# A decoder layer in one kernel: a bias moved into a weight load, two loads swapped, and all instruction orders written anew

## The chip, the cores and the metric

The kernel runs on one core of a Trainium2 chip. A core has a matmul engine (TensorE, PE in the profile), a vector engine (VectorE, DVE), a scalar engine (ScalarE, ACT), a general engine (GpSimd, POOL) and a queue that issues transfers (SyncE, SP). Each runs its own list of instructions in order, and they meet only at semaphores. The metric is the device time of one launch in microseconds (us).

## What is computed

One post-norm decoder layer over 16 batches of 256 rows, 128 wide, in float32:

```python
# 1: linear attention, 16 heads of 8
q = elu(x @ Wq + bq) + 1;  k = elu(x @ Wk + bk) + 1;  v = x @ Wv + bv
k = k / sqrt(sum(k * k) + EPS)
attn = (q @ k.T) @ v                      # per head, no softmax
y = x + attn @ Wo + bo
x = layernorm(x + (layernorm(y) * gamma + beta))
# 2: cross-attention to 64 context rows, 16 heads of 64
p = softmax((x @ Wq_x)(ctx @ Wk_x).T * 64 ** -0.5)
x = layernorm(x + p @ (ctx @ Wv_x) @ Wo_x)
# 3: gated FFN, 352 wide, activations and weights rounded to FP4 by blocks of 16
h = silu(fp4(x) @ fp4(w_gate).T) * (fp4(x) @ fp4(w_up).T)
x = layernorm(x + fp4(h) @ fp4(w_down).T)
```

## The kernel before

The work of a batch b is cut into small calls, each one to sixteen instructions, defined once for their engine and then called in a list that is written out by hand, one list for each engine. Between the calls stand waits on semaphores. Since an engine does its list in order, the list decides which batches overlap.

**Set-up.** The query and key matrices of the cross-attention are folded with the context into one matrix M. `g_product` multiplies the weights per head (TensorE); `g_cut_high`, `g_keep_low` (VectorE) and `g_keep_high` (ScalarE) split the result GT into a high and a low part; `context_cut`, `context_low` (GpSimd) and `context_high` do it with the context, in two halves of 512 columns. `m_product(half, hd)` makes 3 matmuls for head hd and one half of the batches, 32 calls in all, over six PSUM banks; `m_keep` copies the banks away, in turn on ScalarE and VectorE. `hw_product` folds the value and output weights; `weights_...` round the FFN weights, `weights_transpose` and `keep_weights` bring them in place. VectorE's first call `biases` waits for the semaphore `aw_loaded`, which counts the loads of the key and value bias rows (`kv_bias`), the query bias (`bq_col`) and the attention weights (`w_attn`). `keep_warm(bank, n)` makes n matmuls whose result nobody reads; the first such call has n = WARM.

**Attention of batch b.** `project_kv` and `project_q` into bank A2; k's features by `k_exp` and `k_features`, then the inverse root in small steps (`k_sums` to `k_better`), `k_norm` on GpSimd; `kv_outer`, `keep_kvT`, `kv_project`, `keep_kvo`, `attn_out` in bank A1; `attn_residual` and two layer norms. Each layer norm goes `statistics`, `aggregate` (VectorE), `variance_eps`, `minus_mean`, `rstd_of`, `shift_of` (GpSimd), then a norm on ScalarE.

**Cross-attention.** `x1_transpose`, then for each half t of the rows `scores` into the two banks S, `score_max` (VectorE), `scores_shift` (TensorE adds the maximum into S), `softmax_exp` (ScalarE), `fold_halves` (GpSimd), `score_sums` and `score_reciprocals` (VectorE), `probabilities` (GpSimd), `p_transpose` into the banks TP, `keep_pT` (ScalarE) and `cross_out` into A2, with `values` and `keep_vo` once for a batch; then `cross_residual` and a layer norm, whose `cross_norm` writes into one of three x2 buffers and waits for the `ffn_residual` three batches back.

**FFN.** `x_max` to `x_rounded` and `x_dequantise` round the input, `xf_transpose`, `keep_xfT`; `gate_up(b, t)`, `gate_tanh`, `gate_times`, `gated` for each t; `h_max`, `h_reciprocal`, `h_scaled`, `h_magnitudes` (ScalarE), `h_rounded_up`, `h_rounded`, `h_dequantise` (GpSimd), `h_transpose`, `keep_hT`, `down` into A2, `ffn_residual`, layer norm, `store_out`. `gate_up(b, 1)` waits until `gated(b, 0)` has read its banks.

From scores(15, 1) on, TensorE's list reads: scores(15, 1), p_transpose(14, 1), gate_up(11, 0), cross_out(14, 0), h_transpose(10), gate_up(11, 1), p_transpose(15, 0), cross_out(14, 1), scores_shift(15, 1), values(15), xf_transpose(12), keep_warm(A2, 3), down(10), gate_up(12, 0), cross_out(15, 0), h_transpose(11), gate_up(12, 1), p_transpose(15, 1), cross_out(15, 1), xf_transpose(13), down(11), gate_up(13, 0), h_transpose(12), gate_up(13, 1), down(12), xf_transpose(14), gate_up(14, 0), keep_warm(F0, 8), gate_up(14, 1), xf_transpose(15), gate_up(15, 0), h_transpose(13), down(13), gate_up(15, 1), keep_warm(TP0, 4), h_transpose(14), down(14), keep_warm(TP0, 17), h_transpose(15), down(15).

## Time and profile before

| | |
|---|---|
| median of 3 runs | 390.3 us (390.25 to 391.2) |
| the profiled execution | 389.87 us |
| its span, first to last instruction | 387.9 us |
| TensorE busy | 357.9 us (92%), 2113 matmul records |
| VectorE busy | 295.1 us (76%) |
| GpSimd busy | 264.5 us (68%) |
| ScalarE busy | 248.7 us (64%) |

The time of the profiled execution and its span differ by what the launch adds before the first and after the last instruction. A float32 matmul is more than one record in the trace, and ends of matmuls are modelled, so the time that a call takes is read from its start to the start of the next. Transfers carry 26 GB/s over the span, most of it in the first 17 us.

### The profile page before, as it was taken

Reading aid. Unit: us, or ns where it says so; the run is one execution under the profiler, and the core shown is the slowest. Engines: PE = TensorE matmul, PEld = TensorE weight load, DVE = VectorE, ACT = ScalarE, POOL = GpSimd, SP = SyncE. Lnnn points to the kernel's source line nnn. Section 1 sums busy time; section 2 is a strip of 40 time slices with the busy share of each in tenths; the row PEclk is TensorE's granted clock in tenths of the full one; section 3 lists DMA queues with packets and bytes.
Section 4 is the critical chain, followed back from the end, with each engine's and each line's share of the span. In section 5 each row is a group of like instructions: output and inputs, shape, how many; then the busy total and the mean of one; then the engine's idle time right before and its main releaser. Section 6 shows DMA issues by size and latency. Waiting matters only on the chain.

```text
span 387.9 us, 7167 instructions
## 1 busy us (share of the span) xinstructions
PE 357.9 (92%) x2113; PEld 265.9 (69%) x2113; DVE 295.1 (76%) x814; ACT 248.7 (64%) x526; POOL 264.5 (68%) x441
## 2 busy tenths in 40 slices
PE   6499999899999999999999999999999999876782
PEld 6388766567767787577686778685776778664572
DVE  0879566757779897896766969797989788888881
ACT  0657667678668676766876696757666666545422
POOL 3501157998986979799877899788849676624232
PEclk9689999999999999999999999999999999999999
DMA  7810001101000011000000000000000000000000
GB/s 244 258 29 14 3 11 31 29 3 41 14 30 0 15 28 30 13 17 27 27 2 16 1 16 14 3 0 14 15 1 15 1 15 14 3 14 15 14 14 27
DMA packets 13280, 10.42 MB, mean 27 GB/s; under 512 B 1051, under 2 KB 12476, under 8 KB 13244
## 3 DMA queue, kind: packets, MB, share of 16 engines
q1 hardware_dynamic: 12668, 7.89, 7.0%
q10 hardware_dynamic: 576, 2.10, 1.5%
q8 instruction: 17, 0.28, 0.3%
q14 instruction: 19, 0.16, 0.1%
HBM read 7.88 MB, written 2.10 MB: 26 GB/s over the span
## 4 chain that ended last, share of the span: by engine, by line
PE 80%; issue 6%; DVE 5%; ACT 4%; DMA 2%; POOL 1%; SPq 0%; ACTq 0%; POOLq 0%; DVEq 0%
PE A L2589 15%; PE S L2562 14%; PE F L2604 8%; PE TP L2552 7%; PE TP L2580 7%; PE A L2619 4%; PE S L2571 4%; PE A L2513 3%; DMA w_attn<-in_attn_w 2%; PE TP L2491 2%; PE F L2491 2%; PE A L2537 2%; PE TP L2612 2%; PE A L2526 2%; PE S L2491 2%
## 5 line engine op out<-in xcount | busy, mean ns | idle before, releaser
L403 POOL TENSOR_TENSOR pe<-pe,srec 128x1024 f32<-128x1024 f32 x32 | 60.9, 1903 | 9.2 <-DVE srec L1704 9.2
L2589 PEld LDWEIGHTS A<-wvoT,wqkT 128*128 128x128 f32 x512 | 60.4, 192 | 4.4 <-ACT wqkT L987 1.7
L2589 PE MATMUL A<-wvoT,wqkT 128*128 128x128 f32 x512 | 62.2, 276 | 1.1 <-ACT wqkT L987 1.1
L2562 PE MATMUL S<-M,x1T 128*128 128x512 f32 x128 | 61.0, 599 | 0.8 <-ACT x1T L972 0.7
L397 POOL TENSOR_TENSOR fold<-pe 128x512 f32<-128x512 f32 x32 | 40.7, 1273 | 10.4 <-ACT pe L982 10.3
L1693 DVE TENSOR_REDUCE smax<-S 128x16 fp32r<-128x1024 f32 x32 | 39.0, 1218 | 3.6 <-PE S L2562 3.1
L2604 PE MATMUL F<-w_gu,xfT 128*128 128x352 f32 x112 | 38.0, 462 | 0.7 <-ACT xfT L995 0.6
L987 ACT ACTIVATE wqkT<-TP 128x1024 f32<-128x1024 f32 x32 | 32.7, 1023 | 8.7 <-PE TP L2580 8.5
L2562 PEld LDWEIGHTS S<-M,x1T 128*128 128x128 f32 x128 | 22.2, 190 | 21.0 <-issue 18.6
L982 ACT ACTIVATE pe<-S 128x1024 f32<-128x1024 f32 x32 | 32.7, 1021 | 6.0 <-PE S L2571 5.9
L413 POOL TENSOR_TENSOR hv<-hv,ham 128x704 f32<-128x704 f32 x16 | 22.2, 1387 | 17.5 <-DVE hv L1769 17.5
L2580 PE MATMUL TP<-ident,pe 128*128 128x128 f32 x256 | 33.3, 273 | 0.3 <-ACT wvoT L976 0.3
L2580 PEld LDWEIGHTS TP<-ident,pe 128*128 128x128 f32 x256 | 29.2, 141 | 4.7 <-issue 1.3
L2552 PE MATMUL TP<-HW,ctx_f 128*64 128x512 f32 x128 | 31.0, 605 | 0.0
L388 POOL TENSOR_TENSOR kn<-fk,ky 128x256 f32<-128x256 f32 x16 | 11.1, 694 | 27.5 <-DVE ky L1665 27.5
L2619 PEld LDWEIGHTS A<-w_dn,hT 128*128 128x128 f32 x192 | 23.1, 192 | 8.2 <-issue 5.6
L1698 DVE TENSOR_REDUCE ssum<-fold 128x16 f32<-128x512 f32 x32 | 21.8, 680 | 8.2 <-POOL fold L397 8.2
L2619 PE MATMUL A<-w_dn,hT 128*128 128x128 f32 x192 | 24.6, 278 | 3.4 <-ACT hT L1007 3.0
L381 POOL TENSOR_TENSOR xb<-x_sb,rows 128x512 f32<-128x512 f32 x16 | 20.4, 1273 | 10.5 <-DMA rows<-in_attn_rows 8.6
L2604 PEld LDWEIGHTS F<-w_gu,xfT 128*128 128x128 f32 x112 | 19.5, 190 | 9.0 <-issue 1.8
L2571 PE MATMUL S<-smax,ident_r 128*128 128x512 f32 x64 | 23.5, 448 | 1.8 <-DVE smax L1693 1.8
L954 ACT ACTIVATE x<-yx,shift_cross,rstd_cross 128x128 f32<-128x128 f32 x32 | 14.9, 489 | 11.7 <-DVE yf L1774 10.6
(188 smaller groups left out, 870.6 us busy)
## 6 DMA issues: line engine op xcount, KB each, us to landing
xT<-in_x_t SPq DMA_DIRECT2D x16, 128.0 KB, 2.1
x_sb<-in_x SPq DMA_DIRECT2D x16, 128.0 KB, 2.2
out<-yf SPq DMA_DIRECT2D x16, 128.0 KB, 1.8
M<-in_fw SPq DMA_DIRECT2D x1, 560.0 KB, 10.3
wqkT<-in_wq_t ACTq DMA_DIRECT2D x1, 512.0 KB, 4.3
wqkT<-in_wk_t ACTq DMA_DIRECT2D x1, 512.0 KB, 6.3
ctx_f<-in_ctx_t ACTq DMA_DIRECT2D x1, 512.0 KB, 7.9
wvoT<-in_wv_t ACTq DMA_DIRECT2D x1, 512.0 KB, 9.2
```

What stands on the lines that cost most here:

```text
L397: ge.tensor_tensor(by_head(fold[n % 2][:, :]), p4[:, :, 0, :], p4[:, :, 1, :], ALU.add).then_inc(fold_made, 1)
L403: ge.tensor_tensor(w, w, spread(srec[n % 2][:, :], HX, R), ALU.mult).then_inc(pn_made, 1)
L982: sc.activation(pe_[n % NPE][:, :], S[:, :], ACT.Exp, scale=SCALE).then_inc(pe_made, 1)
L987: sc.activation(pT[n % 2], TP[:, :].rearrange("p (a n) -> p a n", a=NJ), ACT.Copy).then_inc(pT_kept, 1)
L1693: ve.tensor_reduce(smax[n % 2][:, :], by_head(S[:, :]), AX.X, ALU.max, negate=True).then_inc(smax_made, 1)
L2552: last = te.matmul(TP[par * R:par * R + R, half * BANK:half * BANK + BANK], ctx_f[:, b * R:b * R + R], HW[:, par, 4 * half:4 * half + 4, : ...
L2562: last = te.matmul(S[:, half * BANK:half * BANK + BANK], x1T[b % 2][:, t * P:t * P + P], M[:, b // BH, HC * half:HC * half + HC, b % BH * ...
L2571: last = te.matmul(S[:, half * BANK:half * BANK + BANK], ident_r[:, :], spread(smax[n % 2][:, HC * half:HC * half + HC], HC, R), start=Fal ...
L2580: last = te.transpose(TP[:, j * P:j * P + P], pe_[n % NPE][:, j * P:j * P + P], ident[:, :])
L2589: last = te.matmul(A2[:, t * P:t * P + P], pT[n % 2][:, j, :], vo[b % 2][:, j, :], start=(j == 0), stop=(j == NJ - 1))
L2604: last = te.matmul(bk[:, 0:I], xfT[b % 2][:, t * P:t * P + P], w_gu[:, m, :], start=True, stop=True)
L2619: last = te.matmul(A2[:, t * P:t * P + P], hT[b % 2][:, t, k * P:k * P + P], w_dn[:, k, :], start=(k == 0), stop=(k == NK - 1))
```

## The change

The query bias is appended to the attention weights as a 513th column and `bq_col` becomes a view of it; its own load is gone. The load of the bias rows stands behind that of w_attn. `m_product` waits for the half of the context that it reads instead of for both. WARM is 18 instead of 12, and `keep_warm(F0, 6)` stands ahead of the first m_product. VectorE also gets a function `scores_shift` that nothing calls.

```diff
-def decoder_layer(nc, x, x_t, attn_w, attn_rows, bq_in, ctx_t, ...):
+def decoder_layer(nc, x, x_t, attn_w, attn_rows, ctx_t, ...):
-        w_attn = sb("w_attn", [P, 4 * P])
+        w_attn = sb("w_attn", [P, 4 * P + 1])
+        bq_col = w_attn[:, 4 * P:4 * P + 1]
-        bq_col = sb("bq_col", [P, 1])
-        WARM = 12
+        WARM = 18
-            sp.dma_start(kv_bias, attn_rows[0:2 * P].partition_broadcast(NBR)).then_inc(aw_loaded, 16)
-            sp.dma_start(bq_col[:, :], bq_in.rearrange("(p a) -> p a", a=1)).then_inc(aw_loaded, 16)
             load_xT(0)
             sp.dma_start(w_attn[:, :], attn_w).then_inc(aw_loaded, 16)
+            sp.dma_start(kv_bias, attn_rows[0:2 * P].partition_broadcast(NBR)).then_inc(aw_loaded, 16)
-            AW = 16 * 3
+            AW = 16 * 2
                 k = 2 * (hd // 2 // 4) + hd % 2
                 pe.wait_ge(g_high, k + 1)
                 pe.wait_ge(g_low, k + 1)
-                pe.wait_ge(c_high, 2)
-                pe.wait_ge(c_low, 2)
+                pe.wait_ge(c_high, half + 1)
+                pe.wait_ge(c_low, half + 1)
             project_kv(0)
-            pe.wait_ge(fk_made, 1)
-            project_q(0)
             pe.wait_ge(g_low, 2)
+            keep_warm(F0, 6)
             m_product(0, 0)
             pe.wait_ge(g_low, 2)
             m_product(0, 1)
+            pe.wait_ge(fk_made, 1)
+            project_q(0)
-        "attn_w": np.concatenate([i[f"L0_attn_W{n}"] for n in "kvqo"], axis=1),
+        "attn_w": np.concatenate([i[f"L0_attn_W{n}"] for n in "kvqo"] + [i["L0_attn_bq"][:, None]], axis=1),
-        "bq": i["L0_attn_bq"],
```

All five lists are written out in another order. They hold the same calls as before, apart from keep_warm: 44 such matmuls before, with WARM, and 57 after. The order of the loads of x and x_t changes from batch 5 on. Some of what moves: the second half of a batch's probabilities and its p_transpose, the attention calls of the first batches, which stood between the first m_products and now stand behind them, and the FFN calls of the first batches, which come later. The last steps of VectorE:

```diff
@@ VectorE, the last steps
             h_rounded_up(14)
+            ffn_residual(13)
             h_rounded(14)
-            ffn_residual(13)
-            statistics("ffn", 13)
             gate_times(15, 1)
-            aggregate("ffn", 13)
             gated(15, 1)
             h_max(15)
             h_reciprocal(15)
             h_scaled(15)
+            statistics("ffn", 13)
+            aggregate("ffn", 13)
+            h_rounded_up(15)
+            h_rounded(15)
             ffn_residual(14)
-            h_rounded_up(15)
             statistics("ffn", 14)
-            h_rounded(15)
             aggregate("ffn", 14)
```

From scores(15, 1) on, TensorE's list reads after the change: scores(15, 1), down(9), p_transpose(14, 1), gate_up(11, 0), scores_shift(15, 1), cross_out(14, 0), gate_up(11, 1), h_transpose(10), cross_out(14, 1), p_transpose(15, 0), down(10), p_transpose(15, 1), xf_transpose(12), cross_out(15, 0), gate_up(12, 0), cross_out(15, 1), gate_up(12, 1), xf_transpose(13), h_transpose(11), gate_up(13, 0), down(11), keep_warm(S0, 5), gate_up(13, 1), keep_warm(TP0, 7), h_transpose(12), down(12), xf_transpose(14), gate_up(14, 0), h_transpose(13), gate_up(14, 1), xf_transpose(15), gate_up(15, 0), down(13), keep_warm(S0, 3), gate_up(15, 1), keep_warm(TP0, 8), h_transpose(14), down(14), keep_warm(TP0, 10), h_transpose(15), down(15).

## Rows read from the trace of the kernel before

**Rows 1.** Busy time of each engine by stretch, with granted clock.

```profile
core 0: us, PE busy (x) PEld busy (x) DVE busy (x) ACT busy (x) POOL busy (x), PEclk, DMA share, GB/s
0.00:18.45 18.45, 9.54 (x64) 8.20 (x65) 7.47 (x21) 5.09 (x10) 8.18 (x27) 0.82 0.81 264
18.45:60.00 41.55, 41.34 (x215) 31.01 (x213) 29.57 (x76) 28.35 (x73) 10.04 (x20) 0.96 0.06 17
60.00:92.00 32.00, 29.09 (x150) 19.63 (x150) 22.07 (x75) 23.24 (x60) 29.44 (x45) 1.00 0.09 26
92.00:300.00 208.00, 207.99 (x1242) 152.62 (x1242) 169.84 (x487) 147.64 (x306) 174.83 (x278) 1.00 0.05 14
300.00:322.90 22.90, 22.32 (x134) 16.50 (x131) 19.86 (x49) 15.53 (x26) 16.28 (x28) 1.00 0.02 7
322.90:387.90 65.00, 47.67 (x319) 37.88 (x317) 46.33 (x111) 28.90 (x54) 25.76 (x47) 1.00 0.05 15
```

**Rows 2.** The chain that ended last, first 24 us: start, length, what.

```profile
2.17 8.73 DMA w_attn<-in_attn_w
```

**Rows 3.** Timeline of the first 22 us, all engines.

```profile
1.29 0.37 SPq L284 DMA_DIRECT2D bq_col<-in_bq  x1
...
2.12 4.36 PE L2626 MATMUL A<-ident 128*128 128x128 f32 x24 [2.12 <-POOL ident L350]
...
7.54 1.16 PE L2471 MATMUL F<-wqkT 64*128 64x128 f32 x16 [1.06 <-DMA wqkT<-in_wk_t]
...
10.92 0.15 DVE L1566 TENSOR_SCALAR bq_col<-bq_col 128x1 f32<-128x1 f32 x1 [9.79 <-DMA w_attn<-in_attn_w]
...
12.38 1.29 DVE L1586 TENSOR_SCALAR pe<-F 128x512 int32<-128x512 int32 x2
...
17.79 1.22 PE L2521 MATMUL A<-xT,w_attn 128*128 128x256 f32 x2 [2.87 <-DVE fk L1641]
...
18.45 3.12 PE L2491 MATMUL F<-ctx_r,GT 128*128 128x512 f32 x6
```

**Rows 4.** Stretches of 1 and 2 us; columns as in rows 1.

```profile
11.00:12.00 1.00, 0.00 (x0) 0.00 (x0) 0.90 (x6) 0.00 (x0) 0.00 (x0) 0.97 1.13 325
22.00:23.00 1.00, 1.00 (x5) 0.79 (x5) 0.79 (x3) 0.36 (x1) 0.00 (x0) 0.91 0.00 0
384.00:386.00 2.00, 0.00 (x0) 0.00 (x0) 0.00 (x0) 0.88 (x2) 0.57 (x2) 1.00 0.00 0
```

**Rows 5.** TensorE's waits, 56 to 92 us: total, times, longest.

```profile
PE S L2571 <- DVE smax L1693: 1.3, 2, 0.9
```

**Rows 6.** Waits of all engines, whole span.

```profile
ACT x L954 <- DVE yf L1774: 10.6, 5, 2.8
```

**Rows 7.** Timeline of TensorE near the end.

```profile
334.98 0.94 PE L2626 MATMUL A<-ident 128*128 128x128 f32 x6 [1.03 <-ACT xfT L995]
335.75 1.50 PE L2619 MATMUL A<-w_dn,hT 128*128 128x128 f32 x12
337.09 1.35 PE L2604 MATMUL F<-w_gu,xfT 128*128 128x352 f32 x4
338.27 1.95 PE L2589 MATMUL A<-wvoT,wqkT 128*128 128x128 f32 x16
340.06 0.82 PE L2612 MATMUL TP<-ident,hv 128*128 128x128 f32 x6
...
344.05 2.05 PE L2589 MATMUL A<-wvoT,wqkT 128*128 128x128 f32 x16 [1.11 <-ACT wqkT L987]
```

**Rows 8.** Timeline of the last 15 us, all engines.

```profile
374.46 3.96 PE L2626 MATMUL TP<-ident 128*128 128x128 f32 x34
374.67 0.42 DVE L1774 TENSOR_TENSOR yf<-A,x 128x256 f32<-128x256 f32 x1 [0.81 <-PE A L2619]
375.01 0.88 DVE L1764 SCALAR_TENSOR_TENSOR hv<-S,hv 128x704 f32<-128x704 f32 x1
...
376.20 0.87 DVE L1769 SCALAR_TENSOR_TENSOR hv<-S,hv 128x704 f32<-128x704 f32 x1
...
377.15 1.39 POOL L413 TENSOR_TENSOR hv<-hv,ham 128x704 f32<-128x704 f32 x1 [4.58 <-DVE hv L1769]
```

More of the change, by code:

```diff
@@ L2033, in _ @@
+            score_reciprocals(5, 1)
             cross_residual(4)
@@ new lines, in _ @@
+            gate_times(6, 0)
+            gated(6, 0)
+            q_features(15)
+            k_guess(15)
+            score_max(12, 0)
+            statistics("post", 13)
+            k_miss(15, 0)
+            gate_times(6, 1)
+            gated(6, 1)
+            h_max(6)
+            h_reciprocal(6)
+            h_scaled(6)
+            k_better(15, 0)
+            ffn_residual(5)
+            aggregate("post", 13)
+            statistics("ffn", 5)
+            h_rounded_up(6)
+            h_rounded(6)
@@ new lines, in _ @@
+            score_max(12, 1)
+            aggregate("ffn", 5)
+            score_sums(12, 0)
+            x_max(8)
+            k_miss(15, 1)
+            score_reciprocals(12, 0)
+            cross_residual(10)
+            k_better(15, 1)
+            x_reciprocal(8)
+            x_scaled(8)
+            statistics("cross", 10)
+            aggregate("cross", 10)
+            x_rounded_up(8)
+            x_rounded(8)
+            gate_times(7, 0)
+            gated(7, 0)
+            keep_kvT(14)
@@ new lines, in _ @@
+            score_sums(12, 1)
+            score_reciprocals(12, 1)
+            gate_times(7, 1)
+            gated(7, 1)
+            h_max(7)
+            h_reciprocal(7)
+            score_max(13, 0)
+            ffn_residual(6)
+            h_scaled(7)
+            statistics("ffn", 6)
+            x_max(9)
+            aggregate("ffn", 6)
+            x_reciprocal(9)
+            x_scaled(9)
+            h_rounded_up(7)
+            h_rounded(7)
+            score_sums(13, 0)
+            x_rounded_up(9)
@@ L2263, in _ @@
+            x_rounded(9)
+            score_max(13, 1)
+            score_reciprocals(13, 0)
+            gate_times(8, 0)
+            gated(8, 0)
+            cross_residual(11)
             attn_residual(14)
@@ L2315, in _ @@
[L2315 to L2326 removed]
+            ffn_residual(8)
+            statistics("ffn", 8)
+            aggregate("ffn", 8)
+            score_sums(14, 0)
+            score_reciprocals(14, 0)
@@ L2835, in _ @@
-            p_transpose(2, 1)
+            cross_out(2, 1)
+            scores_shift(3, 1)
+            pe.wait_ge(pT_kept, 6)
+            values(4)
+            pe.wait_ge(yx_made, 3)
+            xf_transpose(0)
+            pe.wait_ge(pe_made, 8)
+            x1_transpose(4)
+            pe.wait_ge(ky_made, 24)
+            attn_out(5)
+            pe.wait_ge(xfT_kept, 1)
+            project_q(6)
             pe.wait_ge(m_kept["act"], 16)
@@ new lines, in _ @@
+            p_transpose(4, 1)
+            pe.wait_ge(xfT_kept, 3)
+            project_q(8)
+            pe.wait_ge(pe_made, 11)
+            scores(5, 1)
+            pe.wait_ge(h_made, 4)
+            gate_up(2, 0)
+            pe.wait_ge(pT_kept, 10)
+            h_transpose(0)
+            scores_shift(5, 1)
+            pe.wait_ge(fq_made, 9)
+            cross_out(4, 0)
+            cross_out(4, 1)
+            pe.wait_ge(ky_made, 30)
+            kv_project(7)
+            pe.wait_ge(hT_kept, 1)
@@ L2941, in _ @@
-            scores_shift(6, 0)
-            attn_out(9)
+            pe.wait_ge(hT_kept, 2)
+            p_transpose(5, 1)
+            pe.wait_ge(fq_made, 10)
+            cross_out(5, 0)
+            pe.wait_ge(pT_kept, 12)
+            h_transpose(2)
+            cross_out(5, 1)
+            pe.wait_ge(hT_kept, 3)
+            p_transpose(6, 0)
+            pe.wait_ge(yx_made, 6)
+            down(1)
+            pe.wait_ge(pT_kept, 13)
+            values(7)
+            pe.wait_ge(xg_made, 4)
```

2864 lines of the change are left out of this document (1374 added, 1490 removed).

## The prediction

> **What bounds the kernel now.** I read the page's slices first, where TensorE is at 9 tenths from the third to the thirty-third nearly throughout, then its busy time by stretch [rows 1], then its waits, then the first 22 and the last 65 us instruction by instruction. A new order can win in three places alone. From 0 to 18.45 us TensorE does 9.54 us of work, part of it matmuls that only keep the clock up. From 18.45 to 322.9 us it stands idle for 0.21 + 2.91 + 0.01 + 0.58 = 3.7 us in all; more than that no order can win there. From 322.9 us, where scores(15, 1) ends, to the end it is busy 47.7 of 65.0 us, and VectorE 46.3: neither is full, so that stretch is a chain of waits across the engines [rows 1].
>
> **The sum's base.** The profiled execution took 389.87 us, its span 387.9, so 1.97 lie around the span. The median of the runs is 390.3, 0.4 above the profiled one. Terms are counted against 389.87, and the 0.4 is added at the end. About 0.3% (1.2 us) is what a measurement of this kernel can tell from no change.
>
> **The start.** Before, VectorE's biases wait for three transfers on one semaphore; the last is w_attn, issued at 2.17, landed 8.73 us later [rows 2]. VectorE begins at 10.92 [rows 3]. The change takes out one issue of 0.37 us [rows 3] and puts kv_bias behind w_attn. The counter still needs all of the bytes, 289 KB of them, so being first in the queue wins nothing for w_attn alone: I take one issue, 0.4 us; bounds 0 and 0.9 (two issues).
>
> Now TensorE. Before, project_q(0) waited for fk until 17.79, and m_product(0, 0), behind it in the order, ran from about 19.0 [rows 3]. By 22.1 the half clock ended (granted 0.91 from 22 to 23 us; it fell between 11 and 12, granted 0.97) [rows 4]. From 19.0 to 22.1 at half speed is 1.55 us of full-speed work, and project_q(0) is 0.43 more: 1.98. After, m_product(0, 0) needs the first half of the context and g_low 2, and project_q(0) stands behind it. VectorE is the one that it waits for: the biases, from 10.92 to 12.38, took 1.46 us, and six steps of a 512-column tile (two in 1.29 us) follow up to g_keep_low(0, 1) [rows 3]. Starting 0.4 earlier, that is about 16.1. Then come 6 new warm matmuls, 0.23 us each at full clock (17 in 3.96 us [rows 8]): 1.4 us, or 2.8 at half. WARM goes from 12 to 18: 6 at 0.23 make 1.4 us, so they end at 7.9 instead of 6.5, and g_product, at 7.54 before, starts 0.3 later [rows 3]. That costs nothing, since its first reader on VectorE stands behind the biases; without that cover it would be the 0.3.
>
> If the clock falls again at about 12 us, m_product(0, 0) starts at 18.9; with steady work since 16.1, where before it was since 17.8, the clock comes back some 2 us sooner, at 20. By 22.1 that is 0.55 + 2.1 = 2.65, a gain of 0.7. If it does not fall, it starts at 17.5 and has done 4.6: a gain of 2.6. For the fall: TensorE is again idle from 9.6 to 12. Against: this time it has worked without a gap up to 9.6, and at the end the last matmul is over at 382.0 and the clock is still full from 384 to 386 [rows 4]. I cannot settle this and take the middle, **1.6 us**; bounds 0 (the clock returns no sooner) and 2.6. TensorE is busy for 41.34 of the next 41.55 us [rows 1], so what is won there is carried on, provided that VectorE keeps up: it is busy 29.6 of these 41.55, and products and their copies are the same in number.
>
> A rule of the Trainium skill speaks against this part (DMA: Bandwidth & Descriptors, How a descriptor splits into AXI transactions): a descriptor that doesn't start on a 256-byte boundary is read with extra transactions. A row of w_attn becomes 2052 bytes long, so nearly all rows start off a boundary, and by that rule its load lands later, not sooner. I make it an estimate of 0.3 us, and the sum below would be 385.0 by it. No row here shows such a load.
>
> **The middle.** The same calls run on each engine, in another order; nothing is added. Up to score_max(15, 1), softmax_exp(15, 1) and fold_halves(15, 1) VectorE, ScalarE and GpSimd have the same work as before within 3 us, added up from the order and the mean durations. What could be lost are waits. I added up, in both orders, the TensorE work that lies between a step and the next that needs the same PSUM bank. Scores(b, t) to scores_shift(b, t) has to cover a score_max of 1.2 us: it is short in 4 places before (0.9, 0.7, 0.4, 0.4 us; the trace shows two of them as waits for smax, 1.3 us [rows 5]) and in 3 after (0.1, 0.9, 0.4), and scores_shift to the next step on S is short in 2 after (0.5, 0.9). So 2.4 against 2.8. The TP bank is short once before, never after. GpSimd's lead over TensorE at the first p_transposes grows by 2 us. The pre-pass of attention is spread wider: attn_out(6) moves 17 us of TensorE work back. I take **0**; bounds: 3.7 won, and as much lost, a second filling of the pipeline like that from 60 to 92 us (2.9 idle), of which this order has more waits than I can see.
>
> **The end.** A call's time is from its start to the next one's: down 1.34 (335.75 to 337.09), gate_up 1.18, cross_out 1.79 [rows 7]. Count from Z, the end of scores(15, 1) (322.9 before). Up to Z TensorE has 0.5 us more to do in the new order without warm matmuls: values(15), 1.87, is now ahead of it, down(9), 1.34, behind. From Z to the end of cross_out(15, 1) it has before: 3 p_transpose, 4 gate_up, 4 cross_out, 2 h_transpose, values, scores_shift, xf_transpose, down, 3 warm matmuls, in all 20.8 us, and two waits of 1.03 and 1.11 us [rows 7]; that gives 23.0, and the trace shows 23.1. After: h_transpose(11), gate_up(12, 1), values(15) and the warm ones are gone from there, down(9) is added: 17.6 us, and one wait of 0.45 (xf_transpose(12), its copy, cross_out(15, 0), all on one bank): 18.1. So the last batch's cross-attention ends 5.0 us sooner after Z.
>
> From there I followed the four queues, each step at the later of its engine and its input. VectorE's cross_residual(15) at Z + 18.2; gate_up(13, 1) ends at Z + 26.3 (before 30.4), h_rounded(13) at 33.3 (39.0), gate_up(14, 1) at 36.5 (39.9), gate_up(15, 1) at 42.6 (46.7), h_rounded(15) at 48.3 (54.1). VectorE has 27.1 us of work in the last 30.1 of these, against 25.0 in 30.9 before: it comes close to full, since gate_times(12, 1) to h_scaled(12) (2.9 us) now follow cross_residual(15), which eats most of the lead. One piece is sure: before, h_rounded_up(15) stood behind ffn_residual(14), 0.3 us late, and with statistics(14) between them h_rounded(15) started 1.19 us after it, where 0.8 would do [rows 8]. Both now follow h_rounded(15), under GpSimd's 1.39 us h_dequantise(15): 0.7 us. The chain after h_rounded(15) is the same, 10.8 us to the end. On the other side 5 warm matmuls (1.15 us) stand between gated(13, 0) and gate_up(13, 1), where VectorE waits 0.85 us for them; 7, 8 and 10 others lie in waits for GpSimd.
>
> Z to the end is 48.3 + 10.9 = 59.2, for 65.0: 5.8 sooner, less the 0.5 ahead of Z: 5.3. My steps follow one another without handover, the trace's with some 0.05 to 0.08 us (h_rounded(15) ends at 377.07, GpSimd starts at 377.15 [rows 8]). Some 20 such steps make 1.3. So **4.0 us**; bounds 5.3, and 0 if VectorE, nearly full, gives all back.
>
> **Sum.** 389.87 - 1.6 - 0 - 4.0 = 384.3; with 0.4 for the median, **384.7 us**.
>
> **The rivals.**
> *The end gains nothing.* VectorE's 27.1 us meet other short waits, and cross_residual(15) waits behind work that is now ahead of it. For it: its work up to h_rounded(15) is the same in sum, and the lead of 5 us is used at its queue. Against: from Z on it stood idle for 14 us of 54 before. Only the start's 1.6 and the 0.7 of the last rounding are left: 390.3 - 2.3 = 388.0.
>
> *All is given back by equal waits.* The start stays at half clock until 22.1 and the end gains 1 or less: 389.5 to 390.5, no change. For it: the work is equal to the last instruction, and the middle had nothing to win.
>
> *Slower: the ring of three x2 buffers holds ScalarE.* cross_norm(b) waits for ffn_residual(b - 3). In TensorE's order down(0) moves from 115 to 139 us of work, and cross_norm(3) with it, just ahead of keep_pT(5, 1) and softmax_exp(6, 1) in ScalarE's queue. If a down comes late, the exp behind it is late, then the next scores. Before, ScalarE waited for such a residual 5 times, up to 2.8 us [rows 6], with TensorE's work as cover. Without that cover for 13 batches at 0.9 us each, it costs 11.7 of TensorE time, less the 5.6 won: 396; it decides from 0.45 us a batch on. Against: down(0) stands 1.9 us ahead of the scores_shift(6, 1) that softmax_exp(6, 1) needs anyway. More likely a few such waits: 391 to 393.
>
> **How the numbers follow.** Forecast, both ends gain: 0.62, its own range 381.5 to 387. Rival 1: 0.15 (387 to 389). Rival 2: 0.11. Rival 3: 0.12. Faster 0.62 + 0.15 = 0.77, same 0.11, slower 0.12. The range leaves out rivals 2 and 3 in the main: 381.5 to 389.5.
>
> **What the profile after would show.** biases at about 10.5; the first m_product at 17.5 or 18.9, and whether the clock is half between 12 and 20; TensorE idle for 4 us or less from there to Z; Z at about 322; cross_residual(15) some 18 us after Z; h_rounded(15) about 49.5 after Z, with nothing between it and h_rounded_up(15). Wrong would be: a wait of TensorE above 1 us between 60 and 320 us, cross_residual(15) later than Z + 20, or VectorE idle for over 12 us between Z and h_rounded(15).

## The result, and the profile after

The changed kernel takes 386.47 us (median of 4 runs, 385.94 to 387.0) against 390.35 us for the kernel before in the same session (390.25 to 391.2): a ratio of 0.9896, 95% interval 0.9876 to 0.9916. That is 1.8 us above the forecast of 384.7 and inside its range. The profiled execution took 385.94 us, its span 383.9; all terms below are counted against it and against 389.87 before, a difference of 3.9.

I cut the span at four places of TensorE: the first product over the context, the start of scores(0, 0), the start of scores(15, 1), and Z, the end of scores(15, 1). The stretches of the changed kernel, with busy time by engine and the granted clock (the counterpart of rows 1):

```profile
0.00:14.34 14.34, 10.73 (x86) 10.03 (x87) 6.45 (x20) 4.15 (x8) 5.74 (x25) 1.00 0.86 283
14.34:53.10 38.76, 38.39 (x208) 28.91 (x207) 28.18 (x67) 27.09 (x65) 9.61 (x17) 1.00 0.13 39
53.10:180.00 126.90, 124.54 (x721) 88.80 (x720) 96.77 (x297) 92.38 (x203) 109.72 (x174) 1.00 0.07 19
180.00:260.00 80.00, 78.53 (x441) 55.80 (x440) 67.33 (x185) 60.01 (x129) 69.48 (x105) 1.00 0.04 11
260.00:321.20 61.20, 60.93 (x370) 44.33 (x369) 53.25 (x134) 39.63 (x70) 44.82 (x74) 1.00 0.04 10
321.20:383.90 62.70, 46.98 (x324) 39.23 (x322) 48.08 (x115) 29.04 (x56) 26.06 (x49) 0.98 0.06 16
```

The columns are those of rows 1. The clock, behind GpSimd's busy time, was never below 1.00 until the last stretch. The start of the changed kernel, from its timeline (start, length, engine, line; in brackets the idle time before and what ended it):

```profile
1.25 0.42 SPq L284 DMA_DIRECT2D w_attn<-in_attn_w  x1
...
2.12 6.09 PE L2627 MATMUL A<-ident 128*128 128x128 f32 x36 [2.12 <-POOL ident L349]
...
7.94 0.15 DVE L1564 TENSOR_SCALAR bq_col<-w_attn 128x1 f32<-128x1 f32 x1 [6.80 <-DMA rows<-in_attn_rows]
8.14 1.16 PE L2472 MATMUL F<-wqkT 64*128 64x128 f32 x16
...
12.98 1.60 PE L2627 MATMUL F<-ident 128*128 128x128 f32 x12 [1.49 <-DVE GT L1590]
14.34 1.64 PE L2492 MATMUL F<-ctx_r,GT 128*128 128x512 f32 x6
```

VectorE's biases come at 7.94 us where they came at 10.92 [rows 3], and the first product over the context at 14.34 where it came at 18.45. Now all scores matmuls as one row, first and last start in it; the kernel before, then the changed one:

```profile
L2562 PE MATMUL S<-M,x1T x128: 592/592/697, 60.7 to 322.3; 128*128 128x512 f32 x128
```

```profile
L2563 PE MATMUL S<-M,x1T x128: 592/592/697, 53.1 to 320.6; 128*128 128x512 f32 x128
```

This pair says most. The first scores start 7.6 us earlier, the last ones 1.7. (A call is four of these records; the last starts 0.6 before the call ends, so Z is 321.2, for 322.9.) The stretch between the two grew from 261.6 to 267.5 us. The end, from Z to the last instruction, shrank from 65.0 to 62.7.

The end of the changed kernel on TensorE, and under it on VectorE:

```profile
345.75 1.38 PE L2627 MATMUL S<-ident 128*128 128x128 f32 x10 [1.54 <-DVE h L1747]
346.97 1.35 PE L2605 MATMUL S<-w_gu,xfT 128*128 128x352 f32 x4
...
364.42 0.94 PE L2627 MATMUL S<-ident 128*128 128x128 f32 x6 [1.14 <-DVE h L1747]
365.19 1.35 PE L2605 MATMUL S<-w_gu,xfT 128*128 128x352 f32 x4
```

```profile
339.25 0.42 DVE L1713 TENSOR_TENSOR yx<-A,x 128x256 f32<-128x256 f32 x1 [0.21 <-PE A L2590]
...
348.86 0.52 DVE L1743 SCALAR_TENSOR_TENSOR th<-th,S 128x352 f32<-128x352 f32 x1 [1.09 <-ACT th L998]
...
354.61 0.89 DVE L1773 SCALAR_TENSOR_TENSOR hv<-S,hv 128x704 f32<-128x704 f32 x1
...
367.08 0.52 DVE L1743 SCALAR_TENSOR_TENSOR th<-th,S 128x352 f32<-128x352 f32 x1 [0.78 <-ACT th L998]
...
371.34 0.89 DVE L1768 SCALAR_TENSOR_TENSOR hv<-S,hv 128x704 f32<-128x704 f32 x1 [0.15 <-ACT S L1002]
372.27 0.89 DVE L1773 SCALAR_TENSOR_TENSOR hv<-S,hv 128x704 f32<-128x704 f32 x1
```

cross_residual(15) (L1713) starts at Z + 18.05, as forecast. h_rounded_up(15) and h_rounded(15) stand back to back at 371.34 and 372.27. In front of gate_up(13, 1) and gate_up(15, 1) TensorE first runs 10 and 6 records of warm matmuls, after the operand is there, and both times VectorE waits for the tanh behind them, 1.09 and 0.78 us.

### The profile page after: what moved, and what is told of

The parts are those of the page before. It is cut to its first block, busy times and chain, and to the rows that moved or that the text cites. A ratio compares the mean times of both kernels' runs of the same rounds, so it can differ in the third digit from the quotient of the medians.

```text
span 383.9 us, 7207 instructions
## 1 busy us (share of the span) xinstructions
PE 360.1 (94%) x2139; PEld 267.1 (70%) x2139; DVE 300.1 (78%) x814; ACT 252.3 (66%) x526; POOL 265.4 (69%) x441
## 4 chain that ended last, share of the span: by engine, by line
PE 78%; issue 8%; DVE 4%; POOL 4%; ACT 3%; DMA 2%; SPq 0%; POOLq 0%; ACTq 0%; DVEq 0%
PE A L2590 15%; PE S L2563 14%; PE F L2605 8%; PE TP L2581 7%; PE TP L2553 7%; PE A L2620 4%; PE S L2572 3%; PE A L2514 3%; PE F L2492 2%; PE S L2492 2%; PE TP L2492 2%; PE TP L2613 2%; PE A L2527 2%; DMA rows<-in_attn_rows 2%; PE A L2538 2%
## 5 line engine op out<-in xcount | busy, mean ns | idle before, releaser
L2563 PEld LDWEIGHTS S<-M,x1T 128*128 128x128 f32 x128 | 22.3, 190 | 18.1 <-issue 16.1
L2581 PE MATMUL TP<-ident,pe 128*128 128x128 f32 x256 | 33.3, 273 | 0.0
L1702 DVE TENSOR_REDUCE ssum<-fold 128x16 f32<-128x512 f32 x32 | 21.7, 677 | 10.5 <-POOL fold L396 10.4
L387 POOL TENSOR_TENSOR kn<-fk,ky 128x256 f32<-128x256 f32 x16 | 10.1, 632 | 18.7 <-DVE ky L1663 18.7
L953 ACT ACTIVATE x<-x,shift_post,rstd_post 128x128 f32<-128x128 f32 x32 | 14.4, 487 | 11.6 <-POOL shift_post L433 11.5
```

Source lines behind the costliest of these rows:

```text
L2563: last = te.matmul(S[:, half * BANK:half * BANK + BANK], x1T[b % 2][:, t * P:t * P + P], M[:, b // BH, HC * half:HC * half + HC, b % BH * ...
L2581: last = te.transpose(TP[:, j * P:j * P + P], pe_[n % NPE][:, j * P:j * P + P], ident[:, :])
```

## The experiments

Each profile gives the same six readings, so they stand in one table. They are from the one execution that was profiled, which need not be the median one; the last column is the median of all executions. "First M" is the first product over the context, "clock" the granted clock from 12 to 22 us, "stretch" the time from the start of scores(0, 0) to the start of the last scores record, "end" that from Z to the end of the span. All in us.

| kernel | biases | first M | clock | scores(0, 0) | stretch | end | time |
|---|---|---|---|---|---|---|---|
| before | 10.92 | 18.5 | 0.50 | 60.7 | 261.6 | 65.0 | 390.35 |
| changed | 7.94 | 14.3 | 1.00 | 53.1 | 267.5 | 62.7 | 386.47 |
| old_orders_new_loads | 7.14 | 15.8 | 0.66 | 58.9 | 261.6 | 64.9 | 387.83 |
| new_orders_old_loads | 10.67 | 18.3 | 0.66 | 57.6 | 267.4 | 64.1 | 391.46 |
| own_bq_behind | 9.74 | 16.1 | 1.00 | 54.9 | 267.5 | 63.8 | 390.12 |
| rows_ahead | 8.57 | 15.1 | 1.00 | 53.9 | 267.4 | 62.7 | 386.52 |
| warm_12 | 7.74 | 15.2 | 0.83 | 54.6 | 267.4 | 63.9 | 386.55 |
| no_second_warm | 7.55 | 14.4 | 0.83 | 54.9 | 267.4 | 62.7 | 386.17 |
| whole_context | 7.50 | 14.3 | 1.00 | 53.1 | 267.4 | 63.4 | 386.41 |
| no_tail_s_warm | 7.80 | 14.2 | 1.00 | 53.0 | 267.4 | 61.1 | 384.70 |
| start_on_old | 7.39 | 14.5 | 1.00 | 55.5 | 261.2 | 64.9 | 384.57 |
| relieve_act | 7.16 | 13.9 | 1.00 | 52.6 | 267.4 | 62.8 | 385.38 |
| relieve_dve | 7.96 | 14.5 | 1.00 | 53.4 | 267.3 | 62.7 | 386.00 |
| start_and_end_on_old | 7.43 | 14.2 | 1.00 | 55.2 | 261.2 | 64.0 | 382.81 |

The two relieve kernels have one execution each. The kernel before took 390.91, 390.97, 390.46 and 390.32 us beside the four groups of runs.

**Two things that vary between executions.** They stand behind differences in the table that no edit made. The first is the last product, down(15). With the new order of the end it took 1.58 us in six profiled executions and 2.2 to 2.9 in the four whose end is 63.4 us or longer. There the clock had fallen to half just before or in it. The changed kernel, then own_bq_behind:

```profile
376.54 1.58 PE L2620 MATMUL A<-w_dn,hT 128*128 128x128 f32 x12 [0.99 <-ACT hT L1006]
```

```profile
378.33 2.66 PE L2621 MATMUL A<-w_dn,hT 128*128 128x128 f32 x12 [0.99 <-ACT hT L1007]
```

The surplus over 1.58 (0.6, 1.1, 1.1 and 1.3 us) is what those ends have over 62.7, to 0.1 us. In the four profiles with the old end, which has 17 warm matmuls ahead of h_transpose(15) where the new one has 10, down(15) took 1.58 us each time; no run changes that number by itself.

The second is the pace of the first warm matmuls. They begin at 6 or 7 records in a microsecond and go on at 11 or so, at a granted clock of 1.00 throughout, and the change of pace comes at another time in each execution. So 18 of them took from 5.67 us (relieve_act) to 7.17 us (no_second_warm), and the first g_product, behind them, began between 7.72 and 9.21 us. With 12 of them it began at 7.54 or 7.55.

**Loads against orders.** old_orders_new_loads is the kernel before with the load edit alone:

```diff
-            sp.dma_start(kv_bias, ...).then_inc(aw_loaded, 16)
-            sp.dma_start(bq_col[:, :], bq_in...).then_inc(aw_loaded, 16)
             load_xT(0)
             sp.dma_start(w_attn[:, :], attn_w).then_inc(aw_loaded, 16)
+            sp.dma_start(kv_bias, ...).then_inc(aw_loaded, 16)
```

> The kernel before with the load edit alone: the bias as a column of the attention weights, the key and value rows behind them, every order and the 12 warming matmuls as before. Theory 'start': in the changed kernel the biases were made at 7.94 us instead of 10.92, and scores(0,0) ended 7.7 us earlier; if the loads make that, this kernel makes its biases at 8.0 (7.8 to 8.4), begins its first product over the context near 16, and most of the gain that reached the end of the scores is here as well: 386.5 to 388.0 us. Rival 'orders': the new orders carry the gain; old orders give a start that is 3 us earlier back in the waits of 50 to 92 us, and the time is 389.3 to 390.5 us. Should the biases be made at 10.5 or later, the loads were not what moved them.

387.83 us, ratio 0.9926 (0.9899 to 0.9953). The biases came at 7.14 us with every order as before, so the loads alone move them. The stretch is 261.6 us, the same as before to a tenth: old orders passed the start on whole and gave nothing back. The biases came earlier than the theory's 7.8 to 8.4, the time inside its range.

new_orders_old_loads is the other half: the changed kernel with the three loads as they were to one another (load_xT(0), rows, bias, weights).

> The changed kernel with the three loads of before: the bias in a load of its own of 128 four-byte pieces, behind the key and value rows, both ahead of the attention weights. The bias column costs the orders nothing else. Theory 'start': biases at 10.5 to 11, the first product over the context near 17 to 19, and the time 388.3 to 390.0 us, since 3 us of start are gone and the end's 2.1 us stay. Rival 'orders': new orders have room for a late start in their middle (3.8 us were lost there after an early one), so the time is 386.3 to 387.3 us as in the changed kernel.

391.46 us, ratio 1.0012 (0.9994 to 1.0029). Without the new loads, the new orders bring nothing: they are no better than the old ones, and 1.5 us above what I gave the theory at most. In the profiled execution (391.62 us) the last product took 1.3 us longer, at half clock; three of the ten executions, at a mean clock of 0.992 where the rest had 0.981 to 0.988, took 390.1 to 390.3. The rival falls too: there is no room in the new middle, its stretch is 267.4 us whether scores(0, 0) starts at 53.1 or 57.6.

**Which part of the loads.** own_bq_behind gives the bias its own load again, as the last of the three; rows_ahead keeps the bias as a column and issues the rows first.

```diff
             sp.dma_start(w_attn[:, :], attn_w).then_inc(aw_loaded, 16)
             sp.dma_start(kv_bias, ...).then_inc(aw_loaded, 16)
+            sp.dma_start(bq_col[:, :], bq_in.rearrange("(p a) -> p a", a=1)).then_inc(aw_loaded, 16)
```

> The changed kernel, but the bias in its own load of 128 four-byte pieces, issued behind the attention weights and the key and value rows. If the small pieces themselves hold the queues up (theory 'pieces'), the biases are made at 9.5 us or later, and no order of the issues helps; if it is only that the rows and the bias went ahead of the weights (rival 'order of issue'), they are made at 8.0 to 8.6 us, one more issue of about 0.5 us behind. Time by the first 387.0 to 389.5 us, by the second 386.3 to 387.0 us.

> The changed kernel, with the bias as a column, but the key and value rows issued ahead of the attention weights, as before. Theory 'pieces': the rows are only 33 descriptors of 1 KB, the biases are made at 8.0 to 8.4 us and the time is that of the changed kernel, 386.2 to 387.0 us. Rival 'order of issue': the biases are made at 9.5 us or later and the time is 387.0 to 389.5 us.

The small pieces it is. own_bq_behind took 390.12 us (387.89 to 390.82), rows_ahead 386.52. With them last in the order the biases came at 9.74 us, with the rows first but no small pieces at 8.57. 512 bytes cost 1.8 us of the biases' time (9.74 against 7.94) behind the others, and 2.1 ahead of them (10.67 in new_orders_old_loads against 8.57). Of each 0.4 to 0.5 us is that the last load is issued so much later, the one more issue; 1.3 and 1.7 are the transfer. The order of issue has a price too, but a smaller one: 8.57 lies 0.6 us above 7.94, and above all ten kernels with the changed kernel's loads.

The time of own_bq_behind is above the theory's 389.5. Its profiled execution took 388.8 us, 2.9 more than the changed kernel's: 1.8 at scores(0, 0) and 1.1 in the last product. So the load costs some 1.8 us of time, as of the biases; the fastest execution, at a clock of 0.999 throughout, is 1.4 above the changed kernel's median.

The traffic shows where: the last two figures of a row are the busy share of the DMA engines and the GB/s. The kernel before issued the small pieces at 1.29 us [rows 3]:

```profile
3.00:4.00 1.00, 1.00 (x7) 1.00 (x7) 0.00 (x0) 0.00 (x0) 0.93 (x11) 1.00 0.89 295
4.00:5.00 1.00, 1.00 (x6) 1.00 (x6) 0.00 (x0) 0.00 (x0) 0.19 (x3) 1.00 0.43 152
```

The changed kernel in the same two microseconds, without them:

```profile
3.00:4.00 1.00, 1.00 (x7) 1.00 (x7) 0.00 (x0) 0.00 (x0) 0.93 (x12) 1.00 0.97 350
4.00:5.00 1.00, 1.00 (x6) 1.00 (x6) 0.00 (x0) 0.00 (x0) 0.18 (x3) 1.00 1.04 355
```

own_bq_behind, which issues them at 2.18, has its hole later:

```profile
4.00:5.00 1.00, 1.00 (x6) 1.00 (x6) 0.00 (x0) 0.00 (x0) 0.18 (x3) 1.00 1.06 419
7.00:8.00 1.00, 1.00 (x12) 1.00 (x10) 0.00 (x0) 0.00 (x0) 0.00 (x0) 1.00 0.79 234
8.00:9.00 1.00, 1.00 (x15) 0.88 (x15) 0.00 (x0) 0.00 (x0) 0.00 (x0) 1.00 0.70 226
```

new_orders_old_loads, which issues them at 1.70 behind the rows and ahead of the weights, has the deepest:

```profile
6.00:7.00 1.00, 1.00 (x12) 1.00 (x11) 0.00 (x0) 0.00 (x0) 0.00 (x0) 1.00 0.28 84
```

The hole moves with the load, at a lower busy share as well as a lower rate. The trace has a packet of four bytes at 9 ns, which for 128 of them on 16 engines is under 0.1 us: the time is lost between packets, and what an engine does there the trace doesn't show. It is the small size that counts and not the number alone: w_attn is 128 packets too, of 2 KB, and while they ran in rows_ahead, from 5.5 to 8.0 us, the traffic stayed at 383 GB/s and above. The Trainium skill (DMA: Bandwidth & Descriptors, Specifications) says that a transfer needs 512 bytes or more for full rate and that below it the engine reads, modifies and writes; the direction agrees, and it gives no duration that I could hold against the 1.8 us.

**What keeps the clock.** warm_12 sets WARM back to 12. no_second_warm takes the line `keep_warm(F0, 6)` out.

> The changed kernel with 12 warming matmuls ahead of the first product instead of 18. In the changed kernel they run until 8.21 us and the first product starts at 8.14; the transposed key weights were there before (7.54 us in the kernel before), so 12 would let the product start 0.6 us earlier. Theory 'clock unaffected': the granted clock stays 1.00 from 0 to 22 us, scores(0,0) begins 0 to 0.6 us earlier and the time is 385.8 to 386.5 us. Rival 'the 18 hold the clock': with 1.2 us of nothing before the product the clock falls somewhere between 12 and 22 us and the time is 387.5 to 389 us.

> The changed kernel without the six warming matmuls ahead of m_product(0,0); the product then starts as soon as its operand is there, at 13.0 us instead of 14.3. Theory 'they hold the clock': TensorE is idle only from 11.5 to 13.0 us, but without the six the clock of 12 to 22 us falls to half as in the kernel before and with the new loads alone, scores(0,0) begins 1 to 3 us later and the time is 387.5 to 389.5 us. Rival 'they only cost': the clock stays at 1.00, the products over the context start 1.3 us earlier, and since the middle has passed every delay of the start on one for one, the time is 385.0 to 385.8 us.

Both came out both ways. A mean clock is that of the whole execution, so it doesn't say whether the start or the last product had the half clock. The executions of warm_12 took 385.46 and 385.51 us at a mean granted clock of 0.997 and 0.996, 386.55 at 0.989, and 388.3 and 388.72 at 0.985. Those of no_second_warm took 384.79 and 384.97 at 0.998, and 387.36 and 387.59 at 0.993. The four of the changed kernel all had 0.997 or 0.998 and 385.9 to 387.0 us. In the profiled execution of warm_12 TensorE did 0.21 us of work in the last microsecond before the clock fell (the figure behind GpSimd's is the clock):

```profile
12.00:13.00 1.00, 0.21 (x1) 0.21 (x2) 1.00 (x3) 1.00 (x3) 1.00 (x2) 0.98 1.03 293
13.00:14.00 1.00, 1.00 (x6) 1.00 (x6) 1.00 (x3) 1.00 (x4) 1.00 (x1) 0.50 1.11 379
...
17.00:18.00 1.00, 1.00 (x6) 0.85 (x5) 0.56 (x1) 0.47 (x2) 0.09 (x1) 1.00 0.19 50
```

That execution took 388.3 us, 2.4 more than the changed kernel's: 1.5 at scores(0, 0) and 1.1 in the last product.

In no_second_warm TensorE stood idle from 13 to 14 us and the clock fell at 15, with the product already running:

```profile
13.00:14.00 1.00, 0.00 (x0) 0.00 (x0) 1.00 (x3) 1.00 (x3) 1.00 (x1) 1.00 1.11 383
14.00:15.00 1.00, 0.57 (x3) 0.51 (x4) 1.00 (x2) 1.00 (x4) 1.00 (x2) 1.00 1.03 379
15.00:16.00 1.00, 1.00 (x4) 0.81 (x3) 1.00 (x3) 1.00 (x3) 1.00 (x2) 0.51 1.06 324
```

This execution was late before it came to the place of the edit: its 18 warm matmuls held g_product up until 9.21 us, 1.07 later than in the changed kernel.

```profile
2.12 7.17 PE L2627 MATMUL A<-ident 128*128 128x128 f32 x36 [2.12 <-POOL ident L349]
```

GpSimd's split context came that much later too, so the product began at 14.43 and not at 13.0 although nothing stood in front of it. Of the 1.8 us by which scores(0, 0) was later (54.9 against 53.1), the missing six and the half clock account for some 0.7.

By the times, the six in front of m_product(0, 0) cost 1.6 us (386.47 against 384.88, the mean of the two executions at full clock) and save 1.0 where the clock falls (387.48, the mean of the other two), and in the profiled one of these the late start is in that 1.0. The added matmuls are an insurance that about pays its premium: the medians of the three kernels lie within 0.4 us. With both groups in place the clock of 12 to 22 us was 1.00 in every profile with early biases (9.74 us or before). With the old loads it was not: new_orders_old_loads has both groups and 0.66. The clock of 1.00 in the changed kernel's start was not free.

**Half of the context.** whole_context undoes the half wait and, so that it can, issues the second half of the split right behind the first on all three engines, still ahead of x_plus_rows(0).

```diff
-                pe.wait_ge(c_high, half + 1)
-                pe.wait_ge(c_low, half + 1)
+                pe.wait_ge(c_high, 2)
+                pe.wait_ge(c_low, 2)
```

> The changed kernel with every product over the context waiting for both halves of the split context, and the second half's cut, copy and low part issued right behind the first half's on VectorE, ScalarE and GpSimd, as before. With the new loads on old orders the first product waited until 15.8 us for GpSimd's two low parts (2.5 us together). Theory 'half wait pays': the first product begins at 15.5 to 16.5 us instead of 14.3, 1.2 to 2 us later, the warming matmuls ahead of it have run out by then, and the time is 387.5 to 389.5 us (the lower end if the clock holds, the upper if it falls). Rival 'half wait pays nothing': the folded key matrix is what comes last anyway, and the time is 386.2 to 387.0 us.

386.41 us: no difference, against my theory. The low parts of both halves ran on GpSimd from 11.49 to 14.04 us, under the warm matmuls, which ended at 14.29:

```profile
11.49 2.55 POOL L372 TENSOR_TENSOR ctx_r<-ctx_f,pe 128x512 fp32r<-128x512 f32 x2 [7.32 <-DVE pe L1579]
```

With new loads on old orders they stood behind x_plus_rows(0), and TensorE waited for them:

```profile
11.95 1.27 POOL L380 TENSOR_TENSOR xb<-x_sb,rows 128x512 f32<-128x512 f32 x1 [7.77 <-DMA rows<-in_attn_rows]
13.17 2.50 POOL L372 TENSOR_TENSOR ctx_r<-ctx_f,pe 128x512 fp32r<-128x512 f32 x2
...
15.82 2.90 PE L2490 MATMUL F<-ctx_r,GT 128*128 128x512 f32 x6 [0.63 <-POOL ctx_r L372]
```

The half wait by itself pays nothing once GpSimd splits the context ahead of its sums of x and rows. That this order is what pays is read from the two traces; no run moves these calls alone.

**The warm matmuls of the end.** no_tail_s_warm takes out `keep_warm(S0, 5)` and `keep_warm(S0, 3)`.

> The changed kernel without the warming matmuls ahead of gate_up(13,1) (five, 1.2 us before it starts) and ahead of gate_up(15,1) (three, 0.8 us); VectorE waited 1.09 and 0.78 us for what follows these two. Theory 'they cost': the time from the end of the last scores to the end falls from 62.7 us by 1.0 to 1.9 us, the clock of the last 60 us stays about 0.95, and the time is 384.6 to 385.6 us. Rival 'they hold the clock': it falls in the last 40 us, and the time is 386.3 to 388.5 us.

384.70 us, ratio 0.9848 (0.9823 to 0.9872). The end fell from 62.7 to 61.1 us at a clock of 0.99, with the last product at full clock (1.58 us) in both profiles. They cost, and held nothing that the others did not hold.

**Who is late in the middle.** Two kernels take about 6 us of work off one engine between 190 and 260 us, where most of the lead is lost.

```diff
-                sc.activation(vo[b % 2], TP[:, :].rearrange(...), ACT.Copy).then_inc(vo_kept, 1)
+                n = 16 if 8 <= b <= 12 else P
+                sc.activation(vo[b % 2][:, :, 0:n], TP[:, :].rearrange(...)[:, :, 0:n], ACT.Copy).then_inc(vo_kept, 1)
```

relieve_act does the same to h_magnitudes of batches 3 to 6, relieve_dve instead to h_rounded_up and h_rounded of those batches.

> The changed kernel with less work on ScalarE where its TensorE falls behind (190 to 262 us): keep_vo of batches 8 to 12 copies one eighth of its columns and h_magnitudes of batches 3 to 6 takes 16 of each 352, the rest of both left out; some 6 us of ScalarE's time. The stretch from scores(0,0) to scores(15,1) is 267.5 us, 3.8 us longer than on old orders beyond its own work. Theory 'ScalarE is late': the waits there end with its softmax exponential, norm and transposed copy, so the stretch falls to 264.5 to 266.5 us. Rival 'VectorE is late' (36 of 40 us busy from 220 to 260 us): it falls by less than 0.6 us. Third, 'latencies': it is the chain through several engines and not the load of one, and neither this nor the relief of VectorE takes off more than 1 us.

> The changed kernel with less work on VectorE in the same place: h_rounded_up and h_rounded of batches 3 to 6 work on 16 of each 352 columns, the rest left out; some 6 us of VectorE's time. Theory 'VectorE is late': the stretch from scores(0,0) to scores(15,1) falls from 267.5 to 264.5 to 266.5 us. Rival 'ScalarE is late': it falls by less than 0.6 us. Third, 'latencies': less than 1 us in both.

Stretches of 267.4 and 267.3 us: the part of either engine's load that was taken off is not what holds TensorE. It came to some 5 us in each, 4.3 of ScalarE's and 4.2 of VectorE's time between 180 and 260 us, and not to 6. From 180 to 260 us the changed kernel has TensorE busy for 78.53 of 80 us (above). With ScalarE relieved (its busy time is the fourth of the five, 60.01 before) and then with VectorE relieved (67.33 before):

```profile
180.00:260.00 80.00, 78.51 (x445) 56.22 (x444) 67.89 (x185) 55.75 (x128) 69.58 (x106) 1.00 0.04 11
```

```profile
180.00:260.00 80.00, 78.53 (x440) 55.77 (x440) 63.11 (x185) 60.05 (x129) 70.04 (x106) 1.00 0.04 11
```

**The start alone.** start_on_old is the kernel before with the new loads, the wait for half of the context and the new order of the first calls only: on VectorE 12, on ScalarE 11, on GpSimd 4, and on TensorE:

```diff
-        WARM = 12
+        WARM = 18
             project_kv(0)
-            pe.wait_ge(fk_made, 1)
-            project_q(0)
             pe.wait_ge(g_low, 2)
+            keep_warm(F0, 6)
             m_product(0, 0)
             pe.wait_ge(g_low, 2)
             m_product(0, 1)
+            pe.wait_ge(fk_made, 1)
+            project_q(0)
```

> The kernel before with the new loads and with the changed kernel's start alone: 18 warming matmuls, the first two products over the context ahead of the first query projection with six warming matmuls before them, the wait for half of the context, and the new order of the first 12 calls on VectorE, 11 on ScalarE and 4 on GpSimd. All that follows is in the old order. In every kernel so far the stretch from the start of scores(0,0) to the start of scores(15,1) has kept one length within 0.2 us whatever the start was: 261.6 us on old orders, 267.5 on new ones (2.1 us of it is work that the new order puts there). Theory 'the start alone': scores(0,0) starts at 54.5 to 56 us (53.1 plus the 1.6 us of work that old orders have ahead of it), that of scores(15,1) at 316.1 to 317.6, and with the old end of 64.9 to 65.5 us the span is 381.7 to 383.9 and the time 383.7 to 385.9 us, as good as the changed kernel (386.5) or better: the orders behind the start bring nothing of their own. Rival 'new orders are needed to pass it on': old orders give the gain back between 60 and 100 us, the stretch grows to 263 us or more, and the time is 386.5 to 388 us.

384.57 us (383.93 to 385.51), ratio 0.9849 (0.9826 to 0.9872), and each reading where the theory had it. TensorE is full where the changed kernel's is not:

```profile
180.00:260.00 80.00, 79.99 (x481) 58.61 (x480) 63.56 (x192) 58.15 (x127) 67.34 (x103) 1.00 0.03 9
```

So the new loads with the first calls of four lists bring more than with all five lists made anew: the rest of the new orders costs 1.9 us. By spans, 382.2 against 383.9: scores(0, 0) 2.4 earlier, the stretch 6.3 longer, the end 2.2 shorter, which makes + 1.7.

**Both ends on old orders.** start_and_end_on_old adds two edits to start_on_old:

```diff
-            keep_warm(F0, 8)
             gate_up(14, 1)
@@ VectorE, the last steps
             h_scaled(15)
-            ffn_residual(14)
             h_rounded_up(15)
-            statistics("ffn", 14)
             h_rounded(15)
+            ffn_residual(14)
+            statistics("ffn", 14)
             aggregate("ffn", 14)
```

> The kernel of the last run (new loads and new start, all else in the old order; 384.6 us) with two edits at its end: without the eight warming matmuls ahead of gate_up(14,1), which ran from 354.11 to 356.00 us between the product's operand and the product, and with h_rounded_up(15) and h_rounded(15) ahead of ffn_residual(14) on VectorE, the changed kernel's own last order. Taking the changed kernel's warming matmuls off the same path gave 1.8 us back. Theory 'both are on the path': 1.9 us for the matmuls and 0.7 to 0.9 us for the order, so the end after the last scores falls from 64.9 to 62.1 to 62.6 us and the time is 381.6 to 382.3 us. Rival 'the clock pays': without them the clock of the last 30 us falls and the time is 383.5 us or more. Between them, 382.3 to 383.5 us: another wait is next, which the profile would name.

382.81 us (382.71 to 383.2), ratio 0.981 (0.9797 to 0.9824): the fastest of all here, between the theory and its rival. The end fell by 0.9 us, not by 2.3 to 2.8. The product that the warm matmuls stood in front of now ran at half clock:

```profile
353.80 2.70 PE L2603 MATMUL F<-w_gu,xfT 128*128 128x352 f32 x4 [1.82 <-DVE h L1742]
```

In this execution it took 2.70 us where the like of it takes 1.35, so 1.35 of the 1.9 us saved went back. That this is what limits the end is not shown: two of the five executions had a mean clock of 0.998, where the profiled one had 0.991, and at 382.71 and 383.2 us were no faster. Here TensorE had stood 1.82 us idle in front of it, and the clock was 0.50 from 354 to 356. In no_tail_s_warm waits of 1.54 and 1.15 us were each followed by a product at full clock, 1.45 us long.

## Why the prediction was right, and where it was not

The time was 1.8 us above the forecast, but that it came so near is luck: the start won 4.4 us more than forecast, the middle lost 3.8 and the end 2.2 us that were not in it.

| step | forecast | measured |
|---|---|---|
| biases | 10.5 | 7.94 |
| first product over the context | 17.5 or 18.9 | 14.34 |
| clock from 12 to 20 us | open | 1.00 |
| Z | 321.8 | 321.2 |
| cross_residual(15) | Z + 18.2 | Z + 18.05 |
| gate_up(13, 1) ends | Z + 26.3 | Z + 27.0 |
| h_rounded(13) ends | Z + 33.3 | Z + 34.3 |
| h_rounded(15) ends | Z + 49.5 | Z + 52.0 |
| the span ends | Z + 60.5 | Z + 62.7 |

**The start, forecast 1.6 within 0 to 2.6: mis-sized, and outside its bounds.** scores(0, 0) starts 7.6 us earlier. In the new order project_kv(4) (1.16) and kv_outer(3) (0.44) come after it and not ahead of it, so 6.0 us of it is won. The step that failed is "the counter still needs all of the bytes, 289 KB of them, so being first in the queue wins nothing [...] I take one issue, 0.4 us; bounds 0 and 0.9". I counted bytes; the cost was in 128 pieces of four bytes, and it was 1.8 to 2.1 us (own_bq_behind, new_orders_old_loads). The rest of the 3.0 is order of issue, 0.6 (rows_ahead), and what varies between executions: over the ten kernels with the changed kernel's loads the biases came between 7.14 and 7.96. The second part, the clock, I had left open. It held in all four executions with 18 and 6 warm matmuls and early biases, and not in all with either group taken out (warm_12, no_second_warm) or with late biases (new_orders_old_loads): it took both.

The rest of the working was sound. For a clock that holds it had the first product at 17.5 us and a gain of 2.6; the product came at 14.34, 3.2 sooner, and 2.6 + 3.2 is 5.8 of the 6.0 us. Two smaller terms were off. The kernel before had its first product at 18.45 [rows 3] and not at 19.0, which changes the sum by 0.2 us. And the 18 warm matmuls end at 8.2 us and not at 7.9, here without a cost, but in no_second_warm VectorE waited 1.45 us for g_product behind them.

The 0.3 us that I had estimated by the Trainium skill (DMA: Bandwidth & Descriptors, How a descriptor splits into AXI transactions) for rows of 2052 bytes is not isolated by any run. The packets in the traces speak against it: those of w_attn took 84 ns at the median before, with 2048 bytes, and 85 ns with 2052 (128 packets over 16 engines: 10.8 us in sum before, 11.0 in rows_ahead, 11.6 in the changed kernel). And such a load, issued at 1.70 us in rows_ahead, let the biases go 6.87 us later, where that of 2048-byte rows took 8.73 before [rows 2].

**The middle, forecast 0 within 3.7 either way: a loss just outside its bounds.** The stretch is 5.9 us longer. Of this, project_kv(4), kv_outer(3) and values(15) (1.87) less down(9) (1.34) are 2.1 us of work that moved into it; 3.8 are lost. The forecast's reasoning, that the shortfalls of bank covers are 2.4 against 2.8 us and so nothing changes, looked only at one kind of wait. The records show 1.3 us of it as added idle time (4.1 of 268.1 us from 53.1 to 321.2, against 2.8 of 262.1 from 60.75 to 322.9), spread over waits of 0.6 us at most for nine different releasers. The other 2.5 us stand in no idle time; ends of matmuls are modelled, so small waits can be hidden in them. That the loss belongs to the new orders and not to the start is shown (267.3 to 267.5 us in ten kernels, 261.2 to 261.6 in four). That it is not the load of ScalarE or VectorE alone is shown for those pieces that were taken off. Which handovers make it stays open.

Rival 3, the ring of x2 buffers, did not come: ScalarE waits for such a residual less than before (10.6 us in 5 waits [rows 6]):

```profile
ACT x L953 <- DVE yf L1778: 3.6, 4, 2.6
```

**The end, forecast 4.0: half of it came.** From Z it is 2.3 us shorter, where 4.5 stood in the forecast (65.0 to 60.5); the 0.5 us of work ahead of Z is right. The first half of the working held: cross_residual(15) and what led to it is right to 0.15 us, h_rounded(13) to 1.0. After that the lead melted: gate_up(14, 1) should have ended 3.4 us sooner after Z than before and ended 2.0 sooner (at 359.1), h_rounded(15) 4.6 and ended 2.2. The step that failed is "some 20 such steps make 1.3". Without handovers I had h_rounded(15) at Z + 48.3; it came at 52.0, so they and what I had not priced make 3.7. The two groups of warm matmuls make 1.6 of that between them (no_tail_s_warm), of which only the first group's 0.85 us was in my sum. Which waits make the rest stays open.

**The signs and the chances.** None of the three signs of being wrong came: TensorE's longest wait between 60 and 320 us was 0.6 us, cross_residual(15) came at Z + 18.05, and VectorE was idle for 6.1 us between Z and h_rounded(15). They were set too wide to show what went wrong. The last could hardly have come: the kernel before has 9.2 us of idle time there (45.05 busy of 54.2), and not the 14 that the first rival names. Only the idle time of TensorE from the first product to Z, 4.5 us where I had 4 or less, pointed at the middle.

The start's gain was carried through the middle one for one, as "what is won there is carried on" said, in every kernel. What was missing was that the new middle has a price of its own, which new_orders_old_loads shows bare: with old loads nothing is left of the new orders' gains. In its profile scores(0, 0) is 3.1 us earlier than before, of which 1.6 is work that comes later, the stretch 5.8 longer, and the end only 0.9 shorter, as the last product ran 1.3 longer at half clock.

## What to carry to other kernels

When a semaphore counts several loads, look at the size of the pieces that each is cut into and not only at its bytes: a 512-byte column load of four bytes a partition cost 2 us and belongs into a neighbouring tile. When a change orders everything anew, graft its loads and first calls onto the old orders and measure that: here they held more than the whole gain. Warm matmuls between a product and its ready operand are on the path; take each group out alone, and read both the time and the clock, stretch by stretch and in more than one execution.

## What was not expected of the hardware

- With 128 four-byte pieces on the way the traffic of the whole core was 152 GB/s in a microsecond in which it is 355 without them, and 84 in another order; the hole moved with the place of the load.
- Whether the clock falls differed between executions of one kernel: no_second_warm took 384.8 to 385.0 us in two of its four executions and 387.4 to 387.6 in the other two.
- The same last product, behind the same calls, ran in 1.58 us or in up to 2.88, by the clock of that execution. And the first warm matmuls ran at two paces while the granted clock was 1.00.
- In start_and_end_on_old TensorE's clock was 0.50 from 354 to 356 us after 1.82 us of idle time, though TensorE had been busy for 6.07 of the 10 us before. After 1.54 and 1.15 us of idle time in no_tail_s_warm it stayed at 1.00.
